# Degree histogram of a two-layer graph kernel: split of the node number at 64 instead of 128

## The chip, the cores and the metric

The kernel runs on one core of one Trainium2 chip, in one launch. The metric is the device time of that core in microseconds (us). The runs of the kernel before took 2653.13, 2652.24 and 2649.13 us; their median is 2652.24 us.

## The reference, cut to what matters

A graph with 6250 nodes and 100000 edges (`src`, `dst`, sorted by `dst`) goes through two blocks. The first sums edge features into their target nodes and applies a small perceptron. The second is two layers of graph attention. Each layer adds a term that depends on how often a node stands in `src` (self loops are appended, which adds 1 to every node):

```python
deg = segment_sum(ones_like(src), src, num_segments=n)      # n = 6250, src includes one self loop per node
deg = (deg - deg.mean()) / (std(deg, ddof=1) + 1e-06)
pos = xn @ Wpos[l] + bpos[l] + deg[:, None] * Wdeg[l][0] + bdeg[l]
```

The change touches only how `deg`, a histogram of the 100000 values of `src`, is counted.

## The kernel before, in words

The kernel is written by hand, engine by engine, with counting semaphores between the engines. Three stages follow each other: the edge sums (from about 27 to 340 us in the profile), the dense units of the first block (to about 540 us), and the two attention layers (the rest). Node tiles are 128 nodes, so there are NT = 49 of them.

**The edge-sum stage.** Edges are taken in steps of 512 (four sub-blocks of 128), four steps ("slots") to a round, two rounds to a loop body; there are 62 rounds. For every slot an equality mask of 128 edges by 128 nodes (`es_sel`) is built, and TensorE multiplies the edge features with it (L1095, 16 float32 products a round, each run as two instructions, so 32 records). In even rounds VectorE builds the masks of slots 0 and 1, in odd rounds that of slot 1 (L1134); ScalarE builds those of slots 2 and 3 (L1027, L1035), GpSimd that of slot 0 in odd rounds (L1050). VectorE adds each finished slot from PSUM to the aggregate (L1148). The edge features come by one 256 KB DMA a slot (L992, issued by SyncE), into buffers for two rounds.

**The histogram** rides along. `src` lies as 125 rows by 800 columns; each round takes 13 columns (`HIST_ROUND`). VectorE splits each value into its low 7 bits and the rest, and compares both with number lines, which gives one-hot blocks in bfloat16: `oh_lo`, 125 x 128 x 13 (L1124, laid out so that the 128 entries of one column stand 13 elements apart), and `oh_hi`, 125 x 13 x 49 (L1128). At the end of each round TensorE does 13 products (L1100): weights `oh_lo[:, :, c]` (125 x 128), moving `oh_hi[:, c, :]` (125 x 49), accumulated over the whole stage into a 128 x 49 corner of PSUM bank 0. Count of node 128*t + p thus lands in row p, column t, which is node order. The semaphore `hist_oh` tells TensorE that a round's one-hots are there, `hist_mm` tells that a round's products are done; VectorE waits for it before it overwrites the block of two rounds ago.

**Order.** Each engine's program is in order. VectorE in round m does: one-hots low for m+1, add slot 0, one-hots high for m+1, add slot 1, then mask(s) for m+1 between the adds of slots 2 and 3. Between bodies VectorE also does other work ("interludes": tables for the attention stage, weights, statistics of x; the function `between` in `dve_edge_sums`). TensorE in round m does its four slots, each after its masks, its features and the add that frees its PSUM bank, and then the 13 histogram products.

**The end.** After the last round VectorE reads the counts from PSUM, adds 1 (L1197), masks (L1198); TensorE sums them over all nodes (L930), and the mean, the variance and the scaled degree follow. All other engines wait for `hist_mm` only, and start the dense units.

Of the kernel before, what the change touches and what calls it, by code (L numbers as in the profile page):

```python
# [17 lines left out]
ALU = mybir.AluOpType  # L18
# [7 lines left out]
P = 128  # L26
# [10 lines left out]
SHIFT = 7  # L37
# [35 lines left out]
HIST_COLS = E // HIST_ROWS  # L73
HIST_ROUND = -(-HIST_COLS // ES_ROUNDS)
HIST_PAD = HIST_ROUND * ES_ROUNDS


UNIT, BUFS = 4, 4
# [61 lines left out]
def gnn_kernel(nc, A, out):  # L140
# [7 lines left out]
    with ctx:  # L148
# [5 lines left out]
        def sem(name):  # L154
            return ctx.enter_context(nc.semaphore(name))
# [53 lines left out]
        class Area:  # L209
# [5 lines left out]
            def take(self, words, skip=0):  # L215
# [11 lines left out]
        es_sel = area.take(2 * ES_SLOTS * ES_SUB * P).rearrange("p (h s j n) -> p h s j n", h=2, s=ES_SLOTS, j=ES_SUB)  # L227
        es_dist = area.take(ACT_SLOTS * ES_SUB * P).rearrange("p (s j n) -> p s j n", s=ACT_SLOTS, j=ES_SUB)
        oh_lo, oh_hi = [[area.take(-(-n * HIST_ROUND // 2))[0:HIST_ROWS, :].bitcast(BF16)[:, 0:n * HIST_ROUND]
                         for h in range(2)] for n in (P, NT)]  # L230
        oh_lo = [o.rearrange("p (n c) -> p n c", c=HIST_ROUND) for o in oh_lo]
        oh_hi = [o.rearrange("p (c n) -> p c n", c=HIST_ROUND) for o in oh_hi]
        hist_iota = area.take(P * HIST_ROUND // 2).bitcast(BF16).rearrange("p (n c) -> p n c", c=HIST_ROUND)
        tile_iota = area.take(P // 2).bitcast(BF16)
        src_lo, src_hi = [area.take(HIST_PAD // 2)[0:HIST_ROWS, :].bitcast(BF16) for _ in range(2)]
        es_dst = area.take(ES.steps * ES_SUB).rearrange("p (s j) -> p s j", j=ES_SUB)
        edge_words = area.used[0]

# [157 lines left out]
        es_added = sem("es_added")  # L396
        hist_oh = sem("hist_onehots_ready")
        hist_mm = sem("hist_counted")
        s_degdve = sem("degree_parts_ready")
        s_degpow = sem("degree_std_ready")  # L400

# [146 lines left out]
        def dve_prepare(dve):  # L548
            for T in TABLES:
                dve.memset(T.ends, 0)  # L550
            dve.memset(src_i, -1).then_inc(s_ends_zero, 1)
            for T in TABLES:
                last = dve.memset(T.ones_steps, 1.0)
            link(dve, last)
            dve.wait_ge(s_iota, 1)
            dve.tensor_copy(iota_s, iota_i)
            dve.tensor_copy(iota_n[:, :], iota_i[:, 0:P])
            for T in TABLES:
                dve.tensor_copy(T.step_id, step_id_i[:, 0:T.step_chunks])
            dve.tensor_scalar(node_mask[:, :], node_id_i, float(N), None, ALU.is_lt)  # L560
            for i in range(2):
                dve.tensor_scalar(minus_past[:, i:i + 1], node_id_i[:, 0:1], float(i + 1), -1.0, ALU.is_ge, ALU.mult)
            dve.tensor_copy(tile_iota, iota_i[:, 0:P])
            link(dve, dve.tensor_copy(hist_iota, iota_i[:, 0:P].unsqueeze(2).to_broadcast([P, P, HIST_ROUND])))
            dve_steps(dve, ES)
            dve_done(dve, ES, 0, ES.chunks)
            dve_tiles(dve, ES)

            dve.wait_ge(s_start_row, 1)
            dve.tensor_copy(es_start[:, :], row_of(START_BANK)).then_inc(s_start_in, 1)  # L570
            dve.wait_ge(s_issued, 1)
            dve.wait_ge(s_src, 16)
            dve.tensor_scalar(src_i[:, 1, :], src_i[:, 0, :], SHIFT, None, ALU.arith_shift_right)
            link(dve, dve.tensor_scalar(src_i[:, 0, :], src_i[:, 0, :], P - 1, None, ALU.bitwise_and))
            dve.tensor_copy(src_lo, src_i[:, 0, :])
            link(dve, dve.tensor_copy(src_hi, src_i[:, 1, :]))
            dve_node_tiles(dve, ES)
            dve_relative(dve, ES)

            dve.wait_ge(s_relt, 1)  # L580
            dve.tensor_copy(es_nt[:, :], row_of(TILE_BANK)).then_inc(s_es_nt, 1)
            dve.tensor_copy(es_dst.rearrange("p (k s) j -> p k s j", s=P),  # L582
                            bank[:, 6:8, :].rearrange("p b (j s) -> p b s j", s=P)).then_inc(s_tab, 1)
# [328 lines left out]
        def pe_attention_table(pe, n):  # L912
# [8 lines left out]
            if n == 1:  # L921
# [2 lines left out]
                pe.wait_ge(s_wprep, 3 * LAYERS + 1)  # L924
                rows(SRC_BANK, src_f, range(AT.step_chunks))

        def pe_degree_sum(pe, i):

            pe.wait_ge(s_degdve, i + 1)
            pe.matmul(bank[:, DEG_BANK, SUM_AT[i]:SUM_AT[i] + NT], ones_f[:, :], deg_tmp[:, :], start=True, stop=True).then_inc(s_degsum, 1)  # L930
# [149 lines left out]
        def pe_edge_sums(pe):  # L1080
            def body(i, first, last_body):
                for h in range(2):
                    m = i * 2 + h
                    for s in range(0 if last_body and h == 1 else ES_SLOTS):
                        pe.wait_ge(es_in[h * ES_SLOTS + s], 16 * (i + 1))
                        if h == 1 and s == POOL_ODD:
                            pe.wait_ge(es_sel_pool, i + 1)
                        elif s in DVE_SLOTS[h]:
                            pe.wait_ge(es_sel_dve, i * DVE_BODY + h * len(DVE_SLOTS[0]) + DVE_SLOTS[h].index(s) + 1)
                        else:  # L1090
                            pe.wait_ge(es_sel_act, m * ACT_SLOTS + s - ACT_FIRST + 1)
                        if not (first and h == 0):
                            pe.wait_ge(es_added, (m - 1) * ES_SLOTS + s + 1)
                        for j in range(ES_SUB):
                            last = pe.matmul(bank[:, 4 + s, 0:P], es_attr[:, h, s, j, :], es_sel[:, h, s, j, :],  # L1095
                                             start=j == 0, stop=j == ES_SUB - 1)
                        last.then_inc(es_summed, 1)
                    pe.wait_ge(hist_oh, m + 1)
                    for c in range(HIST_ROUND):
                        last = pe.matmul(bank[:, 0, 0:NT], oh_lo[h][:, :, c], oh_hi[h][:, c, :], start=first and h == 0 and c == 0,  # L1100
                                         stop=last_body and h == 1 and c == HIST_ROUND - 1, skip_group_check=True)
                    last.then_inc(hist_mm, 1)

            def between(i):
                if i == 3:
                    pe_steps(pe, AT)
                if i == 6:
                    pe_tiles(pe, AT)
                if i == 12:
                    pe_count_steps(pe)  # L1110
                if i in (17, 19, 21):
                    pe_weights(pe, (i - 17) // 2)
                if i in (25, 27):
                    pe_attention_table(pe, (i - 25) // 2)
            run_rounds(pe, body, between)

        def dve_edge_sums(dve):
            dve.wait_ge(s_tab, 1)

            def codes_of(codes, m):  # L1120
                return codes[:, bass.ds(m * HIST_ROUND, HIST_ROUND)]

            def low_one_hots(m, h):
                return dve.tensor_tensor(oh_lo[h], hist_iota[0:HIST_ROWS, :, :],  # L1124
                                         codes_of(src_lo, m).unsqueeze(1).to_broadcast([HIST_ROWS, P, HIST_ROUND]), ALU.is_equal)

            def high_one_hots(m, h):
                return dve.tensor_tensor(oh_hi[h], tile_iota[0:HIST_ROWS, 0:NT].unsqueeze(1).to_broadcast([HIST_ROWS, HIST_ROUND, NT]),  # L1128
                                         codes_of(src_hi, m).unsqueeze(2).to_broadcast([HIST_ROWS, HIST_ROUND, NT]), ALU.is_equal)

            def select(m, h, s):
                if not (isinstance(m, int) and m < 2):
# [5 lines left out]
            def body(i, first, last):  # L1138
# [12 lines left out]
                for h in range(1 if last else 2):  # L1151
                    m = i * 2 + h
                    if not (first and h == 0):
                        dve.wait_ge(hist_mm, m)
                    low_one_hots(m + 1, 1 - h)
                    add(m, h, 0)
                    high_one_hots(m + 1, 1 - h).then_inc(hist_oh, 1)
                    add(m, h, 1)
                    ahead = () if last else DVE_SLOTS[1 - h]
                    for s in range(2, ES_SLOTS):  # L1160
                        if s - 2 < len(ahead):
                            select(m + 1, 1 - h, ahead[s - 2])
                        add(m, h, s)
            low_one_hots(0, 0)
            high_one_hots(0, 0).then_inc(hist_oh, 1)
            for s in DVE_SLOTS[0]:
                select(0, 0, s)
            dve.wait_ge(s_es_nt, 1)
# [25 lines left out]
            run_rounds(dve, body, between)  # L1194

            dve.wait_ge(hist_mm, ES_ROUNDS)
            link(dve, dve.tensor_scalar(deg[:, :], bank[:, 0, 0:NT], 1.0, None, ALU.add))  # L1197
            dve.tensor_tensor(deg_tmp[:, :], deg[:, :], node_mask[:, :], ALU.mult).then_inc(s_degdve, 1)  # L1198

        def dve_degree_mean(dve):  # L1200
# [1123 lines left out]
        def _(pe):  # L2324
            pe_prepare(pe)
            pe_edge_sums(pe)
            pe.wait_ge(s_w0, 16 * W0_LOADS)
            pe.wait_ge(es_added, ES_DONE)
            pe_degree_sum(pe, 0)
            run_units(pe, pe_dense(pe), pe_between)  # L2330
            pe.wait_ge(s_order, 2)
# [27 lines left out]
```

## Time and profile before

| what | us |
|---|---|
| median of three runs | 2652.24 |
| the profiled execution, its own time | 2650.84 |
| its span in the trace | 2649.1 |
| TensorE busy (share of the span) | 2101.5 (79%) |
| VectorE busy | 1985.9 (75%) |
| ScalarE busy | 1756.6 (66%) |
| GpSimd busy | 1812.2 (68%) |
| mean granted TensorE clock | 0.936 of full speed |

Busy time is the time in which an engine has an instruction at work; PE is TensorE's matmul side, PEld its loading of weights (the two overlap), DVE is VectorE, ACT ScalarE, POOL GpSimd, SP SyncE. [...] Times in rows count from the start of the span.

### The profile page before, as it was taken

Reading aid. Unit: us, or ns where it says so; the run is one execution under the profiler, and the core shown is the slowest. Engines: PE = TensorE matmul, PEld = TensorE weight load, DVE = VectorE, ACT = ScalarE, POOL = GpSimd, SP = SyncE. Lnnn points to the kernel's source line nnn. Section 1 sums busy time; section 2 is a strip of 40 time slices with the busy share of each in tenths; the row PEclk is TensorE's granted clock in tenths of the full one; section 3 lists DMA queues with packets and bytes.
Section 4 is the critical chain, followed back from the end, with each engine's and each line's share of the span. In section 5 each row is a group of like instructions: output and inputs, shape, how many; then the busy total and the mean of one; then the engine's idle time right before and its main releaser. Section 6 shows DMA issues by size and latency. Waiting matters only on the chain.

```text
span 2649.1 us, 60619 instructions
## 1 busy us (share of the span) xinstructions
PE 2101.5 (79%) x13853; PEld 1745.0 (66%) x13854; DVE 1985.9 (75%) x7060; ACT 1756.6 (66%) x4888; POOL 1812.2 (68%) x1968
## 2 busy tenths in 40 slices
PE   6989977756788888888888876677787787788787
PEld 5988943345676776766776664566676666667676
DVE  7898948756788888788888855677677777777775
ACT  5866746555676777776777745567677777677764
POOL 5756435567777777777777735777777777777773
PEclk9999969788999999999999987999999999999998
DMA  6876723333344444344434413333343333333332
GB/s 199 265 218 215 221 64 121 98 101 106 108 120 122 116 122 118 115 121 120 121 115 120 121 56 98 106 110 110 114 114 110 114 114 113 111 113 114 110 114 64
DMA packets 186625, 326.72 MB, mean 123 GB/s; under 512 B 38934, under 2 KB 100435, under 8 KB 186336
## 3 DMA queue, kind: packets, MB, share of 16 engines
q0 software_dynamic: 80208, 216.22, 28.3%
q1 hardware_dynamic: 105392, 106.64, 12.9%
q14 instruction: 220, 1.80, 0.2%
q8 instruction: 69, 1.13, 0.2%
q10 hardware_dynamic: 736, 0.93, 0.1%
HBM read 291.29 MB, written 20.71 MB: 118 GB/s over the span
## 4 chain that ended last, share of the span: by engine, by line
POOL 45%; issue 20%; PE 17%; DVE 9%; DMA 4%; DVEq 2%; ACT 2%; POOLq 1%; ACTq 0%; SPq 0%
POOL arena L2060 44%; PE bank L1095 7%; DMA arena<-kv_rows,idx_stage 4%; PE bank L2151 2%; PE bank L1100 1%; DVE aggregate L2191 1%; DVE arena L2199 1%; PE bank L1787 1%; PE bank L2142 1%; DVE bn L1518 1%; DVE arena L2233 1%; PE bank L1399 1%; POOL norm_stat L1362 1%; PE bank L1793 1%; PE bank L1416 1%
## 5 line engine op out<-in xcount | busy, mean ns | idle before, releaser
L2060 POOL DMA_INDIRECT arena<-kv_rows,idx_stage x1612 | 1526.9, 947 | 558.5 <-issue 478.0
L2151 PE MATMUL bank<-arena 128*128 128x136 f32 x3328 | 603.9, 313 | 252.8 <-DVE aggregate L2191 249.9
L2151 PEld LDWEIGHTS bank<-arena 128*128 128x128 f32 x3328 | 477.2, 204 | 365.2 <-DVE aggregate L2191 272.7
L2142 PE MATMUL bank<-queries,arena 128*128 x3328 | 490.2, 294 | 171.8 <-DVE arena L2219 132.6
L2142 PEld LDWEIGHTS bank<-queries,arena 128*128 128x128 f32 x3328 | 435.1, 203 | 224.9 <-issue 223.2
L2191 DVE TENSOR_TENSOR aggregate<-bank,aggregate 128x136 f32 x1664 | 493.7, 297 | 100.4 <-issue 39.8
L2219 DVE TENSOR_TENSOR arena<-bank,arena 128x512 f32<-128x512 f32 x416 | 287.0, 690 | 369.5 <-DMA arena<-kv_rows,idx_stage 302.7
L2081 ACT ACTIVATE arena<-iota_n,at_negdst 128x128 f32<-128x128 f32 x1664 | 527.9, 395 | 3.5 <-DMA kv_rows<-arena 1.7
L2092 ACT ACTIVATE arena<-bank 128x512 f32<-128x512 f32 x416 | 247.4, 595 | 187.1 <-PE bank L2127 169.2
L2199 DVE TENSOR_TENSOR arena<-arena,bank 128x512 f32<-128x512 f32 x416 | 282.7, 680 | 31.1 <-ACT arena L2108 31.1
L2127 PE MATMUL bank<-ident,arena 128*128 128x128 f32 x1664 | 267.1, 286 | 19.1 <-ACT arena L2086 19.1
L2233 DVE TENSOR_REDUCE arena<-arena 128x32 f32<-128x512 f32 x416 | 281.8, 678 | 0.2
L2086 ACT ACTIVATE arena<-arena 128x512 f32<-128x512 f32 x416 | 262.1, 630 | 14.7
L1095 PE MATMUL bank<-arena 128*128 128x128 f32 x1952 | 242.0, 283 | 21.7 <-DVE aggregate L1148 14.2
L1841 ACT ACTIVATE arena<-bank 128x256 f32<-128x256 f32 (+1 forms) x225 | 84.2, 377 | 250.4 <-PE bank L1787 176.9
L1095 PEld LDWEIGHTS bank<-arena 128*128 128x128 f32 x1952 | 232.3, 198 | 24.8 <-issue 24.2
L2127 PEld LDWEIGHTS bank<-ident,arena 128*128 128x128 f32 x1664 | 212.0, 149 | 22.3 <-issue 13.5
L2107 ACT ACTIVATE bank<-arena 128x32 f32<-128x32 f32 x416 | 79.7, 192 | 203.5 <-DVE arena L2248 145.3
L1050 POOL TENSOR_SCALAR arena<-iota_n,arena 128x128 f32<-128x128 f32 x120 | 103.5, 874 | 100.5 <-PE bank L1095 92.4
L1027 ACT ACTIVATE arena<-iota_n,arena 128x128 f32<-128x128 f32 x488 | 148.7, 387 | 17.9 <-DVE arena L582 17.9
L1035 ACT ACTIVATE arena<-arena 128x512 f32<-128x512 f32 x122 | 76.7, 631 | 84.2 <-PE bank L1095 84.1
L1793 PE MATMUL bank<-arena,w_up 128*128 128x256 f32 (+1 forms) x400 | 111.3, 407 | 2.1 <-ACT arena L1841 0.4
(330 smaller groups left out, 2788.0 us busy)
## 6 DMA issues: line engine op xcount, KB each, us to landing
arena<-in_edge_attr_dram SPq DMA_DIRECT2D x244, 256.0 KB, 3.5
arena<-kv_rows,idx_stage POOLq DMA_INDIRECT x1612
kv_rows<-arena SPq DMA_DIRECT2D x12, 512.0 KB, 3.8
kv_rows<-arena SPq DMA_DIRECT2D x24, 256.0 KB, 2.2
queries<-in_x_dram SPq DMA_DIRECT2D x12, 256.0 KB, 3.9
arena<-in_x_dram SPq DMA_DIRECT2D x12, 256.0 KB, 4.0
x_rows<-arena SPq DMA_DIRECT2D x12, 256.0 KB, 2.9
x_stream<-arena SPq DMA_DIRECT2D x12, 256.0 KB, 2.3
```

What stands on the lines that cost most here:

```text
L1095: last = pe.matmul(bank[:, 4 + s, 0:P], es_attr[:, h, s, j, :], es_sel[:, h, s, j, :], start=j == 0, stop=j == ES_SUB - 1)
L2060: pool.indirect_dma_start(kv[:, n, :], None, kv_dram[l], bass.IndirectOffsetOnAxis(idx_stage[:, half % 2, n:n + 1], 0)).then_inc(Z.kv_in[s ...
L2081: m = act.activation(dist[:, j, :], iota_n[:, :], ACT.Abs, bias=at_negdst[:, bass.ds(step + j, 1)])
L2086: act.activation(sel[:, r % SEL_SLOTS, :, :], dist, ACT.Relu, scale=-1.0, bias=1.0).then_inc(Z.sel, 1)
L2092: act.activation(sel_t[:, r % SELT_SLOTS, :, :], bank[:, ATT_BANK[0][r % 2], :].rearrange("p (j e) -> p j e", j=QUAD), ACT.Copy).then_inc( ...
L2127: m = pe.transpose(bank[:, ATT_BANK[0][r % 2], j * P:(j + 1) * P], sel[:, r % SEL_SLOTS, j, :], ident[:, :])
L2142: m = pe.matmul(bank[:, ATT_BANK[1][r % 2], j * D:(j + 1) * D], sel_t[:, r % SELT_SLOTS, j, :], q_all[:, bass.ds(tiles[j], 1), :].rearrang ...
L2151: pe.matmul(sums_of(j), sel[:, r % SEL_SLOTS, j, :], msg[:, r % 2, j, :], start=True, stop=True).then_inc(Z.sum, 1)
L2191: dve.tensor_tensor(a, sums_of(j), a, ALU.add).then_inc(Z.added, 1)
L2199: dve.tensor_tensor(msg[:, r % 2, :, 0:D].rearrange("p j (h c) -> p j h c", h=HEADS), kv[:, s:s + QUAD, D:2 * D].rearrange("p j (h c) -> p ...
L2219: dve.tensor_tensor(prod[:, r % 2, :, :], bank[:, ATT_BANK[1][r % 2], :].rearrange("p (j d) -> p j d", j=QUAD), kv[:, s:s + QUAD, 0:D], AL ...
L2233: dve.tensor_reduce(a[:, 0, :], prod[:, r % 2, :, :].rearrange("p j (h c) -> p (j h) c", h=HEADS), AX_X, ALU.add).then_inc(Z.att, 1)
```

## The change

The node number is split at 64. The high part then has 98 values and the low part 64. The high one-hots (125 x 98 x 13, strided by 13 as the low ones were) become the weights, the low one-hots (125 x 13 x 64, packed) the moving operand, and the counts accumulate as 98 x 64. VectorE's order becomes: high, add slot 0, low, add slot 1. At the end VectorE copies the 98 x 64 counts into the middle third of a zeroed 98 x 192 tile `hist_sb`, and TensorE brings them into node order by two float32 products against every second column of the identity, with the counts once at the left and once at the right half of a 128 wide weight block. VectorE then reads the 128 x 49 result. One memset of `hist_sb` stands ahead of the first one-hots.

```diff
+HIST_SHIFT = 6
+HIST_LOW = 1 << HIST_SHIFT
+HIST_HIGH = NT * P // HIST_LOW
-                         for h in range(2)] for n in (P, NT)]
-        oh_lo = [o.rearrange("p (n c) -> p n c", c=HIST_ROUND) for o in oh_lo]
-        oh_hi = [o.rearrange("p (c n) -> p c n", c=HIST_ROUND) for o in oh_hi]
+                         for h in range(2)] for n in (HIST_LOW, HIST_HIGH)]
+        oh_lo = [o.rearrange("p (c n) -> p c n", c=HIST_ROUND) for o in oh_lo]
+        oh_hi = [o.rearrange("p (n c) -> p n c", c=HIST_ROUND) for o in oh_hi]
...
+        hist_sb = area.take(3 * HIST_LOW)[0:HIST_HIGH, :]
...
+        def pe_degree(pe):
+            pe.wait_ge(hist_out, 1)
+            for k, o in enumerate((hist_sb[:, HIST_LOW:3 * HIST_LOW], hist_sb[:, 0:2 * HIST_LOW])):
+                last = pe.matmul(bank[:, 0, P:P + NT], o, ident[0:HIST_HIGH, 0:HIST_HIGH].rearrange("p (t k) -> p k t", k=2)[:, k, :],
+                                 start=k == 0, stop=k == 1)
+            last.then_inc(hist_set, 1)
...
-                        last = pe.matmul(bank[:, 0, 0:NT], oh_lo[h][:, :, c], oh_hi[h][:, c, :], start=first and h == 0 and c == 0,
+                        last = pe.matmul(bank[0:HIST_HIGH, 0, 0:HIST_LOW], oh_hi[h][:, :, c], oh_lo[h][:, c, :], start=first and h == 0 and c == 0,
...
-                    low_one_hots(m + 1, 1 - h)
+                    high_one_hots(m + 1, 1 - h)
                     add(m, h, 0)
-                    high_one_hots(m + 1, 1 - h).then_inc(hist_oh, 1)
+                    low_one_hots(m + 1, 1 - h).then_inc(hist_oh, 1)
...
+            dve.memset(hist_sb, 0.0)
...
             dve.wait_ge(hist_mm, ES_ROUNDS)
-            link(dve, dve.tensor_scalar(deg[:, :], bank[:, 0, 0:NT], 1.0, None, ALU.add))
+            dve.tensor_copy(hist_sb[:, HIST_LOW:2 * HIST_LOW], bank[0:HIST_HIGH, 0, 0:HIST_LOW]).then_inc(hist_out, 1)
+            dve.wait_ge(hist_set, 1)
+            link(dve, dve.tensor_scalar(deg[:, :], bank[:, 0, P:P + NT], 1.0, None, ALU.add))
...
             pe.wait_ge(es_added, ES_DONE)
+            pe_degree(pe)
             pe_degree_sum(pe, 0)
```

## Rows read from the trace of the kernel before

**Rows 1.** The page's chain that ended last, shares of the span by line.
```profile
POOL arena L2060 44%; PE bank L1095 7%; DMA arena<-kv_rows,idx_stage 4%; PE bank L2151 2%; PE bank L1100 1%; DVE aggregate L2191 1%; DVE arena L2199 1%; PE bank L1787 1%; PE bank L2142 1%; DVE bn L1518 1%; DVE arena L2233 1%; PE bank L1399 1%; POOL norm_stat L1362 1%; PE bank L1793 1%; PE bank L1416 1%
```

**Rows 2.** Stretches: length; busy PE, PEld, DVE, ACT, POOL; clock; DMA share, GB/s.
```profile
27.00:341.00 314.00, 293.34 (x2870) 287.19 (x2870) 278.28 (x721) 219.41 (x610) 176.46 (x216) 0.98 0.72 224
60.00:134.00 74.00, 74.00 (x790) 73.92 (x789) 65.84 (x159) 59.02 (x165) 50.97 (x66) 1.00 0.84 267
```

**Rows 3.** Timeline of PE, one round (start us, us, engine, line, operation, count).
```profile
40.33 0.91 PE L1100 MATMUL bank<-arena 125*128 125x49 bf16 x13
...
41.08 3.82 PE L1095 MATMUL bank<-arena 128*128 128x128 f32 x32
...
44.74 0.90 PE L1100 MATMUL bank<-arena 125*128 125x49 bf16 x13
```

**Rows 4.** Single lines: durations of their instructions, ns, min/median/max, and forms.
```profile
L1100 PEld LDWEIGHTS bank<-arena x806: 136/158/182, 35.8 to 340.0; 125*128 125x128 bf16 x162
L1100 PE MATMUL bank<-arena x806: 188/218/228, 35.9 to 340.0; 125*128 125x49 bf16 x162
...
L871 PEld LDWEIGHTS bank<-arena,queries x49: 95/96/117, 85.5 to 86.7; 128*128 128x128 bf16 x49
L871 PE MATMUL bank<-arena,queries x49: 163/163/164, 85.5 to 86.7; 128*128 128x2 bf16 x49
...
L2127 PEld LDWEIGHTS bank<-ident,arena x1664: 139/141/231, 541.2 to 2602.6; 128*128 128x128 f32 x185
...
L879 PEld LDWEIGHTS bank<-ident,arena x4: 79/80/82, 10.1 to 23.1; 128*1 128x1 f32 x4
...
L1095 PEld LDWEIGHTS bank<-arena x1952: 186/192/333, 29.6 to 338.3; 128*128 128x128 f32 x196
L1095 PE MATMUL bank<-arena x1952: 272/275/553, 29.6 to 338.4; 128*128 128x128 f32 x196
```

**Rows 5.** Chain that ended last, edge-sum stage alone, 27 to 341 us, shares by line.
```profile
by line: PE bank L1095 60.8%; PE bank L1100 10.0%; issue 7.4%; DVE aggregate L1148 2.8%; DVEq L1139 1.8%; DVE bn L964 1.4%; DVE arena L1124 1.2%; DMA arena<-in_x_dram 0.9%; DVE arena L820 0.7%; DVE norm_stat L968 0.6%; DVEq L1148 0.6%; PE b
```

**Rows 6.** Timeline of DVE: a round's one-hots, and an interlude behind it.
```profile
63.47 1.09 DVE L1124 TENSOR_TENSOR arena<-arena 125x1664 bf16<-125x1664 bf16 x1 [0.35 <-PE bank L1100]
...
64.77 0.81 DVE L1128 TENSOR_TENSOR arena<-arena 125x637 bf16<-125x637 bf16 x1
...
67.64 2.47 DVE L604 TENSOR_SCALAR queries<-arena 128x896 bf16<-128x896 f32 x4
70.03 1.09 DVE L1124 TENSOR_TENSOR arena<-arena 125x1664 bf16<-125x1664 bf16 x1
...
72.16 0.69 DVE L1134 TENSOR_TENSOR arena<-iota_n,arena 128x512 f32<-128x512 f32 x1
```

**Rows 7.** Timeline of PE: the histogram group beside that interlude, and a stall later on.
```profile
71.33 0.92 PE L1100 MATMUL bank<-arena 125*128 125x49 bf16 x13
...
166.13 1.13 PE L1095 MATMUL bank<-arena 128*128 128x128 f32 x8 [2.63 <-DVE aggregate L1148]
...
260.87 4.36 PE L1095 MATMUL bank<-arena 128*128 128x128 f32 x24 [0.35 <-issue]
```

**Rows 8.** Waits of PE in the stage: us in total, times, longest.
```profile
PE bank L1095 <- DVE aggregate L1148: 14.2, 10, 2.9
```

**Rows 9.** Timeline of the stage's first products and of its end.
```profile
29.63 6.46 PE L1095 MATMUL bank<-arena 128*128 128x128 f32 x32 [4.28 <-DVE arena L1134]
...
340.26 0.21 DVE L1197 TENSOR_SCALAR degree<-bank 128x49 f32<-128x49 f32 x1 [1.14 <-PE bank L1100]
340.50 0.21 DVE L1198 TENSOR_TENSOR degree_parts<-degree,node_mask 128x49 f32<-128x49 f32 x1
...
340.86 0.39 PE L930 MATMUL bank<-degree_parts,ones_f 128*128 128x49 f32 x2 [0.64 <-DVE degree_parts L1198]
341.39 0.21 DVE L1202 TENSOR_REDUCE degree_stats<-bank 128x1 f32<-128x49 f32 x1 [0.67 <-PE bank L930]
...
345.02 1.12 PE L1394 MATMUL bank<-ident,arena 128*128 128x128 f32 x4 [3.77 <-ACT arena L1465]
...
356.35 0.69 DVE L1569 TENSOR_TENSOR arena<-bank,arena 128x512 f32<-128x512 f32 x1 [13.79 <-PE bank L1404]
```

More of the change, by code:

```diff
@@ L75 @@
 HIST_PAD = HIST_ROUND * ES_ROUNDS
+HIST_SHIFT = 6
+HIST_LOW = 1 << HIST_SHIFT
+HIST_HIGH = NT * P // HIST_LOW
+assert HIST_LOW * 2 == P and HIST_HIGH == 2 * NT <= P
 UNIT, BUFS = 4, 4
@@ L229, in gnn_kernel @@
         oh_lo, oh_hi = [[area.take(-(-n * HIST_ROUND // 2))[0:HIST_ROWS, :].bitcast(BF16)[:, 0:n * HIST_ROUND]
-                         for h in range(2)] for n in (P, NT)]
-        oh_lo = [o.rearrange("p (n c) -> p n c", c=HIST_ROUND) for o in oh_lo]
-        oh_hi = [o.rearrange("p (c n) -> p c n", c=HIST_ROUND) for o in oh_hi]
-        hist_iota = area.take(P * HIST_ROUND // 2).bitcast(BF16).rearrange("p (n c) -> p n c", c=HIST_ROUND)
+                         for h in range(2)] for n in (HIST_LOW, HIST_HIGH)]
+        oh_lo = [o.rearrange("p (c n) -> p c n", c=HIST_ROUND) for o in oh_lo]
+        oh_hi = [o.rearrange("p (n c) -> p n c", c=HIST_ROUND) for o in oh_hi]
+        hist_iota = area.take(HIST_HIGH * HIST_ROUND // 2).bitcast(BF16).rearrange("p (n c) -> p n c", c=HIST_ROUND)
         tile_iota = area.take(P // 2).bitcast(BF16)
         src_lo, src_hi = [area.take(HIST_PAD // 2)[0:HIST_ROWS, :].bitcast(BF16) for _ in range(2)]
+        hist_sb = area.take(3 * HIST_LOW)[0:HIST_HIGH, :]
         es_dst = area.take(ES.steps * ES_SUB).rearrange("p (s j) -> p s j", j=ES_SUB)
@@ L398, in gnn_kernel @@
         hist_mm = sem("hist_counted")
+        hist_out = sem("hist_copied")
+        hist_set = sem("degree_in_node_order")
         s_degdve = sem("degree_parts_ready")
@@ L563, in dve_prepare @@
             dve.tensor_copy(tile_iota, iota_i[:, 0:P])
-            link(dve, dve.tensor_copy(hist_iota, iota_i[:, 0:P].unsqueeze(2).to_broadcast([P, P, HIST_ROUND])))
+            link(dve, dve.tensor_copy(hist_iota, iota_i[:, 0:HIST_HIGH].unsqueeze(2).to_broadcast([P, HIST_HIGH, HIST_ROUND])))
             dve_steps(dve, ES)
@@ L572, in dve_prepare @@
             dve.wait_ge(s_src, 16)
-            dve.tensor_scalar(src_i[:, 1, :], src_i[:, 0, :], SHIFT, None, ALU.arith_shift_right)
-            link(dve, dve.tensor_scalar(src_i[:, 0, :], src_i[:, 0, :], P - 1, None, ALU.bitwise_and))
+            dve.tensor_scalar(src_i[:, 1, :], src_i[:, 0, :], HIST_SHIFT, None, ALU.arith_shift_right)
+            link(dve, dve.tensor_scalar(src_i[:, 0, :], src_i[:, 0, :], HIST_LOW - 1, None, ALU.bitwise_and))
             dve.tensor_copy(src_lo, src_i[:, 0, :])
@@ L1121, in codes_of, with high_one_hots @@
                 return codes[:, bass.ds(m * HIST_ROUND, HIST_ROUND)]
+            def high_one_hots(m, h):
+                return dve.tensor_tensor(oh_hi[h], hist_iota[0:HIST_ROWS, :, :],
+                                         codes_of(src_hi, m).unsqueeze(1).to_broadcast([HIST_ROWS, HIST_HIGH, HIST_ROUND]), ALU.is_equal)
             def low_one_hots(m, h):
[L1124 to L1129, printed above, removed]
+                return dve.tensor_tensor(oh_lo[h], tile_iota[0:HIST_ROWS, 0:HIST_LOW].unsqueeze(1).to_broadcast([HIST_ROWS, HIST_ROUND, HIST_LOW]),
+                                         codes_of(src_lo, m).unsqueeze(2).to_broadcast([HIST_ROWS, HIST_ROUND, HIST_LOW]), ALU.is_equal)
             def select(m, h, s):
@@ L1163, in body @@
                         add(m, h, s)
-            low_one_hots(0, 0)
-            high_one_hots(0, 0).then_inc(hist_oh, 1)
+            dve.memset(hist_sb, 0.0)
+            high_one_hots(0, 0)
+            low_one_hots(0, 0).then_inc(hist_oh, 1)
             for s in DVE_SLOTS[0]:
```

## The prediction, written before the changed kernel was run

> **What bounds the kernel now.** I read the whole page first. Most of the run is the attention stage, bound by GpSimd's gathers (44% of the chain), and the change does not touch it [rows 1]. So I cut out the stage that holds the histogram. There PE is busy 293.3 of 314 us, DVE 278.3, ACT 219.4, POOL 176.5, and the DMA engines 72% [rows 2]; between 60 and 134 us PE has no gap at all. PE is the bound there, but DVE is at 89%, close behind it. This closeness is what the forecast turns on.
>
> One round in the dense part is 44.74 - 40.33 = 4.41 us: 0.75 us from the first histogram product to the first edge product, and 3.66 us of edge products [rows 3]. So the 13 histogram products cost 0.75 / 13 = 57.7 ns each.
>
> **What sets 57.7 ns.** I compared load records [rows 4]. A load of one column takes 79 ns: this is the fixed part. The histogram's load (128 columns, 13 elements apart, bf16) takes at least 136, so 57 for its columns. A float32 load for a transpose, 128 columns, takes 141: 61. A float32 load for a product takes 192, about twice that. [...] The moving side has only 49 columns: 188 ns against 163 for two columns, 25 ns. Loading and multiplying overlap: an edge product has 192 - 80 = 112 ns of load and 275 - 163 = 112 ns of columns, yet a pair takes 3.66 us / 32 = 114 ns [rows 3, 4]. [...] I take 45.2 ns: 12.5 ns less a pair, 0.1625 us a round.
>
> [...] The value lies at the rate of the same line's own load, the nearest row.
>
> The packed bf16 load of L871 needs only 96 - 79 = 17 ns for 128 columns [rows 4]; our strided 128 columns need 57, as slow as a float32 load. [...]
>
> **PE's saving on the chain.** In the stage's chain the histogram has 10.0% of 314 us, 31.4 us, which at 0.75 us is 42 of the 62 groups [rows 5]. 42 x 0.1625 = 6.8 us would be the gain if nothing came behind. But DVE does. I went through the starts of all L1124 rows (61 of the loop) and all 62 groups of L1100, of which [rows 6, 7] show one place, and asked in each round how long before PE's use DVE has its last mask ready. Example: the interlude at 67.64 pushes the one-hots to 70.03, the mask is ready at 72.16 + 0.69 = 72.85, and PE's slot 1 begins at 71.33 + 0.75 + a quarter of 3.66 = 72.99. The margin is 0.14 us, which is also what is left in the rounds where PE stalls visibly; it is the signal's travel, so the true margin is nothing. A saving made before such a place survives only if DVE itself started earlier by it, that is if it was made before DVE's last wait for a histogram.
>
> Counted so: groups 0 to 6 survive (DVE waits for group 6, 0.35 us [rows 6]), then the tables bind from 70 to 84 us; of the groups from 90 to 136 us five survive; from 137 to 292 us three, at 144.9, 223.3 and 247.7, because there DVE's interludes set the pace and PE stalls ten times for 14.2 us [rows 7, 8], and a stall swallows what PE gained before it. These are 15 groups, 2.44 us. From 288 us on DVE never waits until 335, but has margins of 0.4 to 1.1 us beyond the signal: the tightest (slot 1 of the round after 320.9) lets through 0.40 us; after it the remaining groups and the last two, which run back to back, give 0.72. Sum 3.56, and 0.08 from partly kept ones: **3.6 us**. With a pair of 31 ns the same count gives 5.3 us, with 90 ns it gives -16.7, for a loss isn't capped by DVE.
>
> [...]
>
> **Start.** The memset of 192 columns and the longer second one-hots stand before DVE's first mask, which PE waits for [rows 9]: about 0.2 us for the memset (between 0.1 and 0.3, the small DVE rows), 0.0 for the rest. +0.2 us.
>
> **End.** Copy 0.21, then DVE to PE to DVE: 340.50 to 341.39 is 0.89 with one float32 product (two records); the second product adds 2 x 0.11. So 0.89 + 0.22 = 1.1 us more before L1197. Behind it: on PE, L930 and then L1394, which waits 3.77 us for ACT [rows 9]; on DVE nothing until 356.35, 13.8 us idle. ACT, POOL and SP wait for `hist_mm` only, and don't see it. Cost 0; without the cover 1.1.
>
> **DMA.** A round loads 1 MB; at 4.25 instead of 4.41 us it asks for 4% more. At 84% share and 267 GB/s PE was never late for data [rows 2, 8], so 0.
>
> **Sum.** -3.6 + 0.2 = -3.4 us. The profiled execution took 2650.84 us, which gives 2647.4. It lies 1.4 below the median of the runs, 2652.24; on the scale of the median the forecast is **2648.8 us**.
>
> **Rivals.**
> A. DVE does not bind so tightly (its waits shift with PE's), and the chain's 42 groups all pay: -6.8 + 0.2, 2645.6 us. For it: the chain view puts PE there. Against it: the margins of 0.14 us.
> B. The pair stays at 57.7 ns, because something else than the load's columns sets it: +0.2, 2652.4. Against it: L871's pairs run far faster, 49 in 1.2 us [rows 4].
> C. Slower side: load and multiply don't overlap once the moving operand has 64 columns. [...] Against it: the edge products overlap fully.
> [...]
> E. PE's clock. After some stalls PE ran 24 records in 4.36 us instead of 2.92, at the lower level [rows 7]. Stalls grow by up to 0.3 us; one more such stretch costs 1.5 us: 2650.3, and one fewer gives it back.
>
> **Chances.** Forecast 0.52 (its own range 2646.3 to 2651.3), A 0.12, B 0.13, C 0.10, D 0.07, E 0.06. What this kernel's timing can tell from no change is about 0.2%, 5.3 us. Faster by more: most of A and the edge of the forecast, 0.20. Slower by more: C, D and a little, 0.20. Within: 0.60. The range: 2644.5, the pair of 31 ns or A, up to 2660, which takes in C and leaves D out.
>
> **What would show it.** L1100 to L1095 starts 0.59 us apart instead of 0.75, rounds of 4.25 us in the dense part up to about 60 us; load records near 125 ns; L1124's successor near 0.89 us; the first visible new PE stalls, or 0.1 to 0.6 us of idle, at 70 to 84 and near 300 and 322 us; PE's stalls at 166 and 178 us longer by up to 0.3; the last histogram product 3.4 us earlier; the attention stage of the same length. The forecast is wrong if a group takes 0.75 us or more, if DVE's one-hots exceed 1.9 us a round, or if the last histogram product comes 6 us earlier.

## The result, and the profile after

The changed kernel takes 2717.51 us (median of five runs, 2711.99 to 2721.15), the kernel before 2649.13 (2645.97 to 2653.13): a ratio of 1.0253, 95% interval 1.0239 to 1.0267, or 68 us slower. The prediction was 2648.8 us with a range up to 2660. The profiled execution took 2721.15 us, with a span of 2719.4.

The loss is in the edge-sum stage: its last histogram product comes at 408.5 us instead of 340.0, 68.5 us later, and the whole span is 70.3 us longer. The 1.8 us left are less than the 9 us between the runs of one kernel. These are the changed kernel's stage as the chain that ended last, and its two stretches with busy PE, PEld, DVE, ACT, POOL, the clock and the DMA, to be laid beside [rows 2, 5]:

```profile
by line: PE bank L1110 59.8%; PE bank L1115 35.5%; DMA arena<-in_x_dram 0.8%; PE bank L912 0.7%; PE bank L910 0.6%; PE bank L916 0.4%; PE bank L915 0.4%; PE bank L922 0.4%; PE bank L914 0.4%; PE bank L908 0.3%; PE bank L878 0.3%; DVE arena 
```

```profile
27.00:409.50 382.50, 378.47 (x2870) 374.08 (x2870) 278.99 (x722) 219.51 (x610) 171.97 (x216) 0.98 0.62 184
...
60.00:134.00 74.00, 74.00 (x605) 74.00 (x604) 48.56 (x101) 44.28 (x123) 36.98 (x47) 0.98 0.65 196
```

The histogram products have gone from 10.0% of 314 us to 35.5% of 382 us. PE is now busy in 378.5 of 382.5 us, while DVE has fallen from 65.8 to 48.6 us of the 74 shown: it waits. The histogram's loads, and one round of PE, in the changed kernel (answering to [rows 3, 4]):

```profile
L1115 PEld LDWEIGHTS bank<-arena x806: 252/268/274, 36.5 to 408.4; 125*98 125x98 bf16 x162
...
48.25 2.35 PE L1115 MATMUL bank<-arena 125*98 125x64 bf16 x13
50.43 3.82 PE L1110 MATMUL bank<-arena 128*128 128x128 f32 x32
```

From 48.25 to 50.43 are 2.18 us for 13 products: **168 ns a pair** instead of 57.7. The edge products still take 3.66 us, so the round is 5.84 us. The load record of 98 columns is 268 ns, against 158 for 128 columns before. If all 62 groups paid, the loss would be 62 x 1.43 = 88.7 us; the first histogram product to the last is 371.9 us instead of 304.1, 67.8 more. Most of the missing 21 us were idle time of PE before. All its waits in the changed kernel's stage are these (total, times, longest):

```profile
PE bank L1110 <- DVE arena L1149: 4.4, 1, 4.4
PE bank L1110 <- issue: 0.2, 1, 0.2
```

The 4.4 us stand ahead of the first product, as 4.28 did before [rows 9]. Between the first and the last histogram product PE was idle for 17.4 us before and is idle for 0.2 now: the 14.2 us of waiting for DVE's adds [rows 8] and 3.2 us of "issue" are gone, because a slower PE is never ahead of DVE. The other 3.7 us are not accounted for; the granted clock in this stretch is 0.99 instead of 0.98. DVE's one-hots, the changed kernel's two lines (ns, min/median/max), and the end of the stage:

```profile
L1139 DVE TENSOR_TENSOR arena<-arena x62: 810/875/952, 27.9 to 400.7; 125x1274 bf16<-125x1274 bf16 x62
...
L1143 DVE TENSOR_TENSOR arena<-arena x62: 1006/1015/1058, 28.6 to 402.0; 125x832 bf16<-125x832 bf16 x62
```

```profile
408.87 0.23 DVE L1213 COPY arena<-bank 98x64 f32<-98x64 f32 x1 [4.08 <-PE bank L1115]
...
409.24 1.06 PE L938 MATMUL bank<-ident,arena 98*128 98x49 f32 x4 [0.41 <-DVE arena L1213]
...
410.34 0.21 DVE L1215 TENSOR_SCALAR degree<-bank 128x49 f32<-128x49 f32 x1 [1.24 <-PE bank L938]
...
413.68 1.11 PE L1412 MATMUL bank<-ident,arena 128*128 128x128 f32 x4 [2.16 <-ACT arena L1483]
```

Together the one-hots take 1.89 us, within the 1.9 us that the prediction allows them. The new step at the end costs 1.47 us (408.87 to 410.34), and PE still waits 2.16 us for ACT behind it, so it is hidden.

### The profile page after: what moved, and what is told of

The parts are those of the page before. It is cut to its first block, busy times and chain, and to the rows that moved or that the text cites. A ratio compares the mean times of both kernels' runs of the same rounds, so it can differ in the third digit from the quotient of the medians.

```text
span 2719.4 us, 60629 instructions
## 1 busy us (share of the span) xinstructions
PE 2198.7 (81%) x13857; PEld 1844.9 (68%) x13858; DVE 1986.9 (73%) x7062; ACT 1756.9 (65%) x4888; POOL 1807.5 (66%) x1968
## 3 DMA queue, kind: packets, MB, share of 16 engines
q8 instruction: 69, 1.13, 0.2%
## 4 chain that ended last, share of the span: by engine, by line
POOL 51%; PE 20%; issue 19%; DVE 5%; DMA 3%; ACT 1%; DVEq 1%; POOLq 1%; ACTq 0%; SPq 0%
POOL arena L2078 50%; PE bank L1110 8%; PE bank L1115 5%; DMA arena<-kv_rows,idx_stage 2%; PE bank L2169 1%; DVE arena L2217 1%; DVE bn L1536 1%; PE bank L1417 1%; PE bank L1805 1%; POOL norm_stat L1380 1%; PE bank L1434 1%; ACT arena L1483 1%; PE bank L1422 1%; DVE aggregate L2209 0%; DVE arena L1556 0%
## 5 line engine op out<-in xcount | busy, mean ns | idle before, releaser
L2104 ACT ACTIVATE arena<-arena 128x512 f32<-128x512 f32 x416 | 262.1, 630 | 14.7
L1115 PE MATMUL bank<-arena 125*98 125x64 bf16 x806 | 145.5, 332 | 0.0
```

What stands on the lines that cost most here:

```text
L1115: last = pe.matmul(bank[0:HIST_HIGH, 0, 0:HIST_LOW], oh_hi[h][:, :, c], oh_lo[h][:, c, :], start=first and h == 0 and c == 0, stop=last_bo ...
L2104: act.activation(sel[:, r % SEL_SLOTS, :, :], dist, ACT.Relu, scale=-1.0, bias=1.0).then_inc(Z.sel, 1)
```

## The experiments

**Theory W (width times stride).** Two prices multiply. One is for columns far apart: 128 of them took 57 ns to load at 26 bytes and 17 ns packed [rows 4]. The other is for a width other than 128, and the rows of before have no bf16 load that shows it; the theory assumes it, because the load of 98 columns took 268 ns and that of 128 took 158. Before, by this theory, the stride made the load longer and the width of 128 made it shorter; the change took away only the second. It takes both prices for a factor of about four, which was an estimate; the runs below measure 3.8 for each (168 / 44.6 and 221 / 57.7 ns a pair). **Rivals:** the 64 moving columns or a lost overlap (M); the number 98 alone (N); the stride alone, whatever the width (S), by which 128 columns would take 168 x 128 / 98 = 219 ns a pair.

In the expectations a fast load is one as L871's, 17 ns for 128 columns beyond the 79 of a single one [rows 4], and an ordinary load is one without this gain. The 4 ns that some of them add to a pair are my estimate, and no run shows them by themselves. The 163 and 82 ns beside them are estimates as well: the strided pair without these 4 is 168 - 4 = 164, and the packed one taken twice is 2 x (44.6 - 4) = 81.

One thing is needed to read the numbers: experiments 1 to 4 ran on one chip, and 5, 6, 9 and 10 on another, on both of which the kernel before takes some 900 us longer (3571 and 3514 us, at a mean granted clock of 0.79 to 0.80 instead of 0.94), with runs up to 0.8% off their median. The edge-sum stage is within 2% of the first chip's, so I read these experiments from the stage. 7, 8, 11 and 12 ran on a chip like the first. Experiments 3, 5, 6, 7 and 8 are one run each (3680.36, 3502.90, 3511.86, 2660.46 and 2721.91 us), so only their traces are used.

**1. Width back to 128, stride kept.**

```diff
-  matmul(bank[0:HIST_HIGH, 0, 0:HIST_LOW], oh_hi[h][:, :, c], oh_lo[h][:, c, :])   # 98 weight columns
+  matmul(bank[:, 0, 0:HIST_LOW],           oh_hi[h][:, :, c], oh_lo[h][:, c, :])   # oh_hi 128 wide, 30 columns zero
```

`hist_sb` takes the place of the used-up low values here, and its memset stands behind the last round.

> The changed kernel, with the weight block widened from 98 to 128 columns (30 zero columns, result rows 98 to 127 unused); stride of 13 elements, 64 moving columns and the end stay. The end's memset moves behind the last round. [...] Rival M (64 moving columns, or loading and multiplying no longer overlapping, costs the time): the pair stays near 168 ns and the time near 2717. [...]

Its histogram loads and a round of PE:

```profile
L1116 PEld LDWEIGHTS bank<-arena x806: 136/159/179, 36.3 to 345.6; 125*128 125x128 bf16 x162
...
49.62 0.91 PE L1116 MATMUL bank<-arena 125*128 125x64 bf16 x13
50.37 3.82 PE L1111 MATMUL bank<-arena 128*128 128x128 f32 x32
```

49.62 to 50.37 is 0.75 us, 57.7 ns a pair, with 64 moving columns. The ratio to the kernel before is 0.9977 (0.9953 to 1.0). Thirty useless columns took the whole loss away: M and S fall, and the width of 128 is worth almost a factor of 3 against 98 at this stride (168 / 57.7). From the first to the last histogram product are 309.3 us.

**2. Stride away, width 98 kept.**

```diff
-  oh_hi[h][:, :, c]
+  oh_hi[h] flattened, [:, c * HIST_HIGH:(c + 1) * HIST_HIGH]
```

> The changed kernel, but TensorE reads its 98 weight columns packed (98 neighbours of the block instead of every 13th element); the counts are then not node degrees. All else stays. [...] Rival N (the number 98 alone makes it slow): 168 ns, 2717 us. Rival M: 168 ns too.

```profile
L1115 PEld LDWEIGHTS bank<-arena x806: 125/126/127, 34.9 to 341.3; 125*98 125x98 bf16 x162
...
47.66 0.74 PE L1115 MATMUL bank<-arena 125*98 125x64 bf16 x13
48.24 3.82 PE L1110 MATMUL bank<-arena 128*128 128x128 f32 x32
```

0.58 us a group, 44.6 ns a pair: the number 98 alone isn't slow, N falls. This is the pair that I had predicted (45.2). First to last histogram product is 306.3 us, 3.0 less than in experiment 1 on the same chip. The time's ratio, 0.9984 (0.9967 to 1.0002), can't tell a gain of 3.4 us.

**3. The kernel before with one column less.**

```diff
-  matmul(bank[:, 0, 0:NT],   oh_lo[h][:, :, c],   oh_hi[h][:, c, :])
+  matmul(bank[0:w, 0, 0:NT], oh_lo[h][:, 0:w, c], oh_hi[h][:, c, :])   # w = 127, for c == 0 128
```

> The kernel before, with one weight column less (127 of 128) in 12 of the 13 histogram products of a round; the first keeps 128. Node 127 of each tile is then not counted in them. [...] Rivals M, and that only the smaller share of the array matters: 57 ns a pair, no change, 2649 us.

```profile
L1101 PEld LDWEIGHTS bank<-arena x806: 136/319/322, 35.0 to 466.5; 125*127 125x127 bf16 x149, 125*128 125x128 bf16 x13
...
47.91 2.88 PE L1101 MATMUL bank<-arena 125*128 125x49 bf16 x13
50.62 3.59 PE L1095 MATMUL bank<-arena 128*128 128x128 f32 x30
```

2.71 us for the group; less one pair of 58 ns, 221 ns for each of the twelve. One column fewer makes the product almost four times as long. Rival M falls once more, and so does the one that only the share of the array in use matters.

The stage was slower than the longer groups explain. From the first to the last histogram product are 431.3 us, 122 more than in experiment 5; 62 x (2.71 - 0.75) = 121.5 us more of products, less the 18.3 us that PE was idle in experiment 5, would be 103. PE was never idle in the 431.3 us, but its granted clock was 0.92, against 0.97 in experiment 5. For example, the edge products took 3.82 us from 92.28 us at a granted clock of 1.00, and 5.44 us from 84.28 us at 0.69. PE had been busy without a gap before both, the histogram's slow loads among its work.

**4. The kernel before with packed weights.**

```diff
-  oh_lo[h][:, :, c]
+  oh_lo[h] flattened, [:, c * P:(c + 1) * P]
```

> The kernel before, but TensorE reads its 128 weight columns packed instead of 13 elements apart; the counts are then not node degrees. VectorE's work stays. Theory W: the load is fast and packed, as that of L871 (17 ns); a pair is set by its 49 moving columns or by the smallest distance seen, 25 ns: group 0.33 us, round 3.98 us in the dense part; with VectorE's margins capping it, 5.7 us less than before, 2643 us; if every group on the chain pays, 42 x 0.42 = 18 us less, 2631. Rival: the load of before was an ordinary one, then 57.7 ns stay and 2649 us.

```profile
L1100 PEld LDWEIGHTS bank<-arena x806: 95/96/100, 36.0 to 342.7; 125*128 125x128 bf16 x162
...
44.05 0.50 PE L1100 MATMUL bank<-arena 125*128 125x49 bf16 x13
44.40 3.82 PE L1095 MATMUL bank<-arena 128*128 128x128 f32 x32
```

0.35 us, 26.9 ns a pair, and a load record of 96 ns as that of L871 [rows 4]. So the stride did cost before: 57.7 against 26.9. The total's ratio, 0.9975 (0.9955 to 0.9995), can mean a gain of 2 or of 16 us, so the stage has to decide: 42 groups on the chain would give 42 x 0.40 = 17 us, but first to last histogram product is 306.6 us, 2.7 less than in experiment 1 on the same chip, and no less than in experiment 2, whose pairs are 18 ns longer. DVE caps it, and the features come late at times; PE's waits in this stage (4.3 of the 8.4 us stand ahead of the first product, as in every run):

```profile
PE bank L1095 <- DVE aggregate L1148: 20.1, 11, 3.3
PE bank L1095 <- DVE arena L1134: 8.4, 6, 4.3
PE bank L1095 <- issue: 8.1, 22, 1.2
PE bank L1095 <- DMA arena<-in_edge_attr_dram: 2.0, 3, 1.3
```

**5. The kernel before again**, for its trace on such a chip.

> The kernel before, unchanged, for its trace beside those of this call. Both theories: histogram pair 57.7 ns, round 4.41 us, first to last histogram product 304 us as in the trace shown, if this chip runs the stage as the first did.

From 34.9 to 344.2 us, 309.3 between the first and the last histogram product, against 304.1 on the first chip and 309.3 in experiment 1. So the 128 columns of experiment 1 restore the stage too. The count of the prediction gave 3.6 for experiment 2 (3.0 measured) and 5.7 for experiment 4 (2.7); these are single traces.

**6 to 8. How far apart is far?** The changed kernel with its 98 columns 2, 4 and 8 elements apart:

```diff
-  oh_hi[h][:, :, c]
+  oh_hi[h] flattened, [:, c:c + s * HIST_HIGH:s]      # s = 2, 4, 8
```

> The changed kernel, but TensorE reads its 98 weight columns 2 elements (4 bytes) apart instead of 13 (26 bytes); the counts are then not node degrees. Theory W1 (any step between columns costs the factor 4): 168 ns a pair, as in the changed kernel. Theory W2 (cost grows with the bytes between columns, up to the factor 4): two times the packed load, 82 + 4 = 86 ns.

> The changed kernel, but TensorE reads its 98 weight columns 4 elements (8 bytes) apart; the counts are then not node degrees. At 4 bytes the pair took 47 ns as packed, at 26 bytes 168. Theory B1 (the cost grows in proportion to the bytes beyond 4, up to the factor 4): two times, 86 ns a pair, group 1.1 us. Theory B2 (a step above 4 bytes costs the full factor at once): 168 ns. Theory B3 (only long steps cost): 45 to 47 ns.

> As the run with 4 elements, but 8 elements (16 bytes) apart; the counts are then not node degrees. Theory B1: the full factor 4 is reached, 168 ns. Theory B2: 168 ns. Theory B3: 45 to 47 ns.

The load records of the three, in this order:

```profile
L1115 PEld LDWEIGHTS bank<-arena x806: 123/126/129, 35.8 to 343.1; 125*98 125x98 bf16 x162
```

```profile
L1115 PEld LDWEIGHTS bank<-arena x806: 165/188/190, 34.9 to 353.3; 125*98 125x98 bf16 x162
```

```profile
L1115 PEld LDWEIGHTS bank<-arena x806: 258/277/278, 35.0 to 409.6; 125*98 125x98 bf16 x162
```

Less the 79 ns of a load of one column [rows 4] they are 47, 109 and 198 ns at the median. The groups take 0.59, 1.13 and 2.26 us: pairs of 45, 87 and 174 ns. Against the packed pair of 44.6 ns the step of 4 bytes is free, 8 bytes cost about double (87), 16 four times (174 / 44.6 = 3.9), and 26 bytes cost no more (168). This is B1 of the later two expectations: the cost grew with the bytes between columns up to a factor of 3.9. Both theories of experiment 6 missed, W1 (168 ns) and W2 (86 ns), since a step of 4 bytes cost nothing (45 ns). Only bf16 was tried, so whether bytes or elements count isn't shown, nor why the cost stops there.

**9. Operands exchanged.** The packed low block as weights, the strided high one moving:

```diff
-  matmul(bank[0:HIST_HIGH, 0, 0:HIST_LOW], oh_hi[h][:, :, c], oh_lo[h][:, c, :])
+  matmul(bank[0:HIST_LOW, 0, 0:HIST_HIGH], oh_lo[h][:, c, :], oh_hi[h][:, :, c])
```

The two products at the end are changed to match, and the memset is left out. My theory W here took the stride for harmless on the moving side: a pair of 45 ns, as the 98 packed weight columns of experiment 2 took, and a last histogram product 3.6 us earlier than before.

> The changed kernel with the operands exchanged: the 64 packed low one-hots are the weights, the 98 strided high ones move; counts accumulate as 64 x 98, and two products put them in node order. VectorE's work stays, without the memset. [...] Rival P (the stride costs the moving side the same factor): 163 + 4 = 168 ns, round 5.84 us, 68 us slower than before.

```profile
L1115 PEld LDWEIGHTS bank<-arena x806: 106/129/154, 35.0 to 429.2; 125*64 125x64 bf16 x162
...
47.34 2.49 PE L1115 MATMUL bank<-arena 125*64 125x98 bf16 x13
49.76 3.84 PE L1110 MATMUL bank<-arena 128*128 128x128 f32 x32
```

2.42 us a group, 186 ns a pair, and a ratio of 1.0215 (1.0184 to 1.0247) to the kernel before: the moving side pays for the step too, somewhat more than rival P's 168 ns. My theory of a harmless moving side was wrong. The ratio allows 65 to 87 us of loss; first to last histogram product is 394.4 us, 85 more than in experiment 5.

**10. VectorE's gain against TensorE's loss.** L1124 compares 1664 elements in 1.09 us, 0.66 ns each, and L1128 637 in 0.81 us, 1.27 ns each [rows 6]; the shorter time per element is the double rate of the expectations. The kernel before, with the high one-hots laid out as the low ones, so that L1128 can have it too:

```diff
-        oh_hi = [o.rearrange("p (c n) -> p c n", c=HIST_ROUND) for o in oh_hi]
+        oh_hi = [o.rearrange("p (n c) -> p n c", c=HIST_ROUND) for o in oh_hi]
...
-  matmul(bank[:, 0, 0:NT], oh_lo[h][:, :, c], oh_hi[h][:, c, :])
+  matmul(bank[:, 0, 0:NT], oh_lo[h][:, :, c], oh_hi[h][:, :, c])
...
-  tensor_tensor(oh_hi[h], tile_iota[..., 0:NT] over HIST_ROUND, codes over NT, ALU.is_equal)
+  tensor_tensor(oh_hi[h], hist_iota[..., 0:NT, :], codes over NT, ALU.is_equal)
```

> [...] Theory D (VectorE's margins bind half of the stage): L1128 falls from 0.82 to 0.55 us, TensorE's pair stays 57.7 ns, and the time falls by 6 us (0.2%), though TensorE saves nothing. Rival: TensorE alone is the bound, then nothing changes. Rival P (stride on the moving side costs four times): 49 columns take 82 ns, 86 a pair, 0.37 us more a round, some 16 us slower.

```profile
L1100 PEld LDWEIGHTS bank<-arena x806: 136/140/145, 35.8 to 353.0; 125*128 125x128 bf16 x162
...
45.51 1.39 PE L1100 MATMUL bank<-arena 125*128 125x49 bf16 x13
46.72 3.77 PE L1095 MATMUL bank<-arena 128*128 128x128 f32 x32
```

L1128 falls from 0.82 to 0.51 us, 0.80 ns an element, but the pair goes to 1.21 / 13 = 93 ns. The ratio is 1.0016 (0.9996 to 1.0036); first to last histogram product 317.2 us, 7.9 more than experiment 5. I had priced the moving side's loss at 86 ns a pair, near enough, and the time at 16 us more, which the ratio excludes. Of PE's added 62 x 0.46 = 28.5 us, 13.0 were swallowed by its idle time, which fell from 18.3 to 5.3 us. Why the stage grew by 7.9 us and not by the 15.5 that are left isn't shown. VectorE's gain may have a part in it, but no run has the strided moving operand without the faster comparison. Theory D, 6 us less, is wrong in its condition: the pair did not stay at 57.7 ns.

**11 and 12. Versions meant to beat both.** Lay the one-hots out in pairs: two neighbouring values of c side by side, then the next entry. A product's columns then stand 4 bytes apart, and VectorE, which runs along neighbours, should keep its double rate. A round takes 14 columns instead of 13, so that they pair up.

```diff
+HIST_ROUND += HIST_ROUND % 2
-        oh_lo = [o.rearrange("p (n c) -> p n c", c=HIST_ROUND) for o in oh_lo]
+        oh_lo, oh_hi = [[o.rearrange("p (g n k) -> p g n k", g=HIST_ROUND // 2, k=2) for o in oh] for oh in (oh_lo, oh_hi)]
...
-  matmul(bank[:, 0, 0:NT], oh_lo[h][:, :, c], oh_hi[h][:, c, :])
+  matmul(bank[:, 0, 0:NT], oh_lo[h][:, c // 2, :, c % 2], oh_hi[h][:, c // 2, :, c % 2])
```

> [...] By the width and stride theory a pair takes 25 to 31 ns, the group 0.36 to 0.43 us, VectorE's two compares 1.16 + 0.56 = 1.72 us instead of 1.90; with VectorE's margins and stalls counted the stage is 16 us shorter, 0.45% of this chip's time. If VectorE doesn't keep the double rate on runs of two elements (2 us and 0.86 us), the stage is DVE-bound and some 40 us longer. If the stage is bound by TensorE alone, it is 24 us shorter.

> The changed kernel (98 weight columns, 64 moving) with the same two edits: 14 columns a round, columns of a product 4 bytes apart. [...] The stage is 10 to 11 us shorter than before, 58 us or more shorter than the changed kernel, which shows that the stride together with the width was the whole loss. If anything else in the change cost time, it stays longer than before.

The version with 128 columns, and behind it the changed kernel with the same two edits:

```profile
L1100 PEld LDWEIGHTS bank<-arena x868: 96/97/103, 35.9 to 325.4; 125*128 125x128 bf16 x174
...
48.08 0.54 PE L1100 MATMUL bank<-arena 125*128 125x49 bf16 x14
48.46 2.03 PE L1095 MATMUL bank<-arena 128*128 128x128 f32 x16
```

```profile
L1115 PEld LDWEIGHTS bank<-arena x868: 124/127/131, 34.6 to 326.1; 125*98 125x98 bf16 x174
...
47.59 0.82 PE L1115 MATMUL bank<-arena 125*98 125x64 bf16 x14
48.25 4.11 PE L1110 MATMUL bank<-arena 128*128 128x128 f32 x32
```

VectorE's two comparisons in the version with 128 columns (busy us, mean ns of one, by form):

```profile
L1125 DVE TENSOR_TENSOR arena<-arena 125x1792 bf16<-125x1792 bf16 x62 | 67.6, 1091 | 13.0 <-issue 6.7 <-PE bank L1100 2.4 <-DVE queries L660 0.8
...
L1125 DVE TENSOR_TENSOR arena<-arena 125x686 bf16<-125x686 bf16 x62 | 31.4, 506 | 0.0
```

They take 1.60 us, less than the 1.72 expected. With 128 columns: 0.38 / 14 = 27 ns a pair, 2631.9 us against 2648.29 of the kernel before on the same chip, ratio 0.9940 (0.9927 to 0.9953), 16.4 us less; 16 were expected. With 98 columns: 0.66 / 14 = 47 ns, 2636.18 us, ratio 0.9957 (0.9944 to 0.9971), 12.1 us less; 10 to 11 were expected. The split at 64 is harmless once the columns stand close together, and even then the split at 128 has the shorter pair, with load records of 97 ns against 127; the two totals' intervals overlap.

Most of both gains seems to come from VectorE. Experiment 4 had the same pair of 27 ns as the version with 128 columns, but comparisons of 1.92 us a round instead of 1.60. Between the first and the last histogram product PE was busy for 271.9 us there and 267.4 us here, yet idle for 34.7 us there and 22.0 us here: the stretch was 2.7 us shorter than before there, and is 14.7 us shorter here (289.4 instead of 304.1). Likewise the pairs of 45 to 47 ns gave 3.0 us in experiment 2 and 12.7 us with the paired layout. The runs are on different chips and a round has one more product here, so the shares are estimates.

## Why the prediction was wrong, point by point

- **The bound.** Right: PE bound the dense part, with DVE close behind.
- **Load and multiply overlap, and the load limits.** Right as a form: with 64 moving columns in both, 98 packed weight columns give a pair of 44.6 ns and 98 at 26 bytes one of 168.
- **The pair of 45.2 ns: this step failed.** No run shows this term for 98 strided columns: it was my estimate, the changed kernel showed 168 ns, and only the packed columns of experiment 2 showed 44.6. The gain of 3.6 us in the sum was counted from it; the stage lost 67.8 us. I read the strided load's 57 ns as the ordinary rate, because a float32 transpose's load took 61, and concluded that the load had no gain from its width, so that nothing could be lost. But two factors were in it. The stride of 26 bytes costs a pair of 98 columns 168 / 44.6 = 3.8, and at that stride a pair of 128 columns is 221 / 57.7 = 3.8 times faster than one of 127. The packed pair of 98 columns taken up to 128 is 44.6 x 128 / 98 = 58 ns, an estimate; times 3.8 for the stride and divided by 3.8 for the width it is 58 again, next to the 57.7 measured. The row that spoke was beside it: L871 has the same width and type, differs in its stride (and in 128 rows instead of 125), and needs 17 ns instead of 57 [rows 4]. Experiment 4 shows that the stride makes this difference. A difference in one property is that property's price; an agreement with a row that differs in three is none.
- **The width.** 127 columns took 221 ns a pair where 128 took 58 (experiment 3), and 98 took 168 where 128 took 57.7 (experiment 1). The chances have such a loss as D, with 0.07 and +17 us. Its 90 ns a pair, an estimate, priced the width without the stride.
- **The bounds.** No run shows the 31 ns of the lower end. The upper 90 ns came from a product's float32 load, 112 ns for 128 columns beyond the 80 of one [rows 4], which isn't strided. It bounded the width, not the stride, so the range was too narrow on the slow side.
- **DVE's margins.** That a gain of PE alone is mostly lost to DVE holds; the count itself is only roughly right. For the measured loss, 88.7 us less PE's 17.4 us of idle time is 71; 67.8 were measured. For the last two versions 16 and 10 to 11 us were counted, and 16.4 and 12.1 measured. For experiment 3 it is 121.5 less 18.3, or 103 us, and 122 were measured, at a granted clock of 0.92 instead of 0.97. For a saving of 3.4 us no total here is sharp enough, and only single traces speak for it (3.0 in experiment 2). Experiment 4 gained 2.7 us where 5.7 were counted; PE waited for its features there too, which the count leaves out.
- **Rival A** (all 42 groups on the chain pay) falls by experiment 4: 17 us of stage would have gone, 2.7 did.
- **Rival B** (the pair stays at 57.7 ns) and **rival C** (load and multiply no longer overlap) fall by experiment 2, with 44.6 ns, and by experiment 1, where 64 moving columns left the pair at 57.7 ns. Rival E, one more stretch like that of 4.36 us, where the granted clock was 0.65, is far too small for 68 us.
- **DVE, start and end.** Right: 1.89 us of one-hots, the high ones 0.875 where 0.89 was foreseen, a memset of 0.22 us at the start, and 1.47 us at the end, covered by PE's wait of 2.16 us for ACT. The end's step was priced 0.4 us too low. Nothing tests by itself what the new order of VectorE's work did.

## What to carry to other kernels

Before a bf16 weight block is narrowed, look at two numbers: has it 128 columns now (at 26 bytes 127 took 221 ns a pair where 128 took 58), and how many bytes apart are its columns. In these runs bf16 columns 4 bytes apart cost no more than packed ones: 98 weight columns 45 against 44.6 ns a pair, and 27 against 26.9 with 128 weight and 49 moving columns both in pairs. A layout in pairs gives that and leaves VectorE its double rate (1792 elements in 1.09 us). Then ask which engine the saving reaches: the same pair of 27 ns gave 2.7 us of stage alone, and 14.7 us together with VectorE's shorter comparisons. Where a load's time equals a known rate, ask whether two factors cancel, and compare with a row that differs in one property only.

## What the runs showed of the hardware

- bf16 weights, time of a load-and-multiply pair: 128 packed 27 ns; 128 at 26 bytes 57.7; 127 at 26 bytes 221; 98 packed or at 4 bytes 45 to 47; 98 at 8 bytes 87; at 16 bytes 174; at 26 bytes 168.
- The moving operand pays too: 49 columns at 26 bytes 93 ns a pair (beside 128 strided weight columns), 98 columns 186 (beside 64 packed ones). At 4 bytes 49 moving columns cost nothing extra: 27 ns a pair with both operands in pairs.
- PE's granted clock fell while PE had no gap: 0.92 over 431.3 us in which it was busy throughout with loads of 127 columns, against 0.97 in the kernel before on such a chip.
- VectorE's comparison kept its shorter time per element with runs of two elements: 1792 elements took 1.09 us (0.61 ns each) and 686 took 0.51 (0.74), where in the kernel before 1664 elements took 1.09 (0.66) and 637 took 0.82 (1.28).
